# Shared down products of four expert layers as three fp32r products

## The reference, cut to what matters

```
g = einsum('bsh,hi->bsi', x, gate_w)
u = einsum('bsh,hi->bsi', x, up_w)
return einsum('bsi,ih->bsh', gelu(g, approximate=True) * u, down_w)   # h = 128, i = 512
```

## Time and profile before

| what | value |
|---|---|
| median of 3 runs | 1442.39 us (1441.62 to 1445.08) |
| the profiled execution | 1442.76 us |
| its span, first to last instruction | 1440.9 us |
| PE busy | 1248.3 us, 87% |
| DVE busy | 856.1 us, 59% |
| ACT busy | 710.7 us, 49% |
| POOL busy | 269.1 us, 19% |
| mean granted clock of PE | 0.96 of full speed |

### The profile page before, as it was taken

How to read it: one execution, slowest core, us unless ns; L and a number is a source line. 1 busy time by engine, 2 the same in 40 slices (tenths; PEclk the granted TensorE clock), 3 DMA queues, 4 the chain that set the end, 5 groups by cost and what they waited for, 6 DMA issues and landing times.

```text
span 1440.9 us, 26352 instructions
## 1 busy us (share of the span) xinstructions
PE 1248.3 (87%) x9301; PEld 967.7 (67%) x9301; DVE 856.1 (59%) x1800; ACT 710.7 (49%) x1385; POOL 269.1 (19%) x454
## 2 busy tenths in 40 slices
PE   4799960678988889998988999989999998998989
PEld 2455620346877779887777888589888854456867
DVE  4878669654445466657776445466564566664242
ACT  1556668545445434444444445333434376665554
POOL 1899200000001213330000003043320111100000
PEclk9899985799999999999999999999999999999999
DMA  8000010211050213212205200123120000000000
GB/s 304 1 2 2 2 73 0 116 81 59 1 198 10 90 56 102 56 29 96 110 1 210 88 1 25 48 80 88 36 94 1 1 1 2 2 2 1 0 15 15
DMA packets 42607, 75.71 MB, mean 53 GB/s; under 512 B 3817, under 2 KB 33521, under 8 KB 41585
## 3 DMA queue, kind: packets, MB, share of 16 engines
q1 hardware_dynamic: 38384, 65.62, 12.5%
q0 software_dynamic: 4096, 8.40, 2.0%
HBM read 59.72 MB, written 14.29 MB: 51 GB/s over the span
## 4 chain that ended last, share of the span: by engine, by line
PE 67%; DVE 15%; ACT 9%; issue 5%; POOL 2%; DVEq 1%; DMA 1%; ACTq 0%; SPq 0%; POOLq 0%
PE bank L1635 7%; PE bank L1624 7%; PE bank L1620 6%; PE bank L1679 5%; PE bank L1413 3%; PE bank L1479 3%; PE bank L1689 3%; PE bank L1611 3%; PE bank L1418 3%; PE bank L1420 2%; PE bank L1419 2%; PE bank L1604 2%; PE bank L1606 2%; PE bank L1605 2%; PE bank L1529 2%
## 5 line engine op out<-in xcount | busy, mean ns | idle before, releaser
L1872 ACT ACTIVATE SC<-bank 128x512 f32<-128x512 f32 x192 | 114.1, 596 | 220.4 <-PE bank L1620 130.3
L1959 DVE SCALAR_TENSOR_TENSOR SC<-bank,SM,SC 128x512 f32<-128x512 f32 x128 | 95.9, 749 | 142.6 <-PE bank L1624 119.7
L2549 POOL DMA_INDIRECT xs<-CC,POSI x64 | 63.6, 994 | 536.1 <-DVE POSI L2353 234.0
L1635 PE MATMUL bank<-A,SC 128*128 x1024 | 137.1, 277 | 10.5 <-DVE SC L1959 9.6
L1624 PE MATMUL bank<-X,SC 128*128 128x128 f32 x1024 | 137.3, 277 | 6.1 <-DVE SC L2234 5.8
L1620 PE MATMUL bank<-X,SC 128*128 128x128 f32 x1024 | 137.5, 278 | 2.0 <-ACT SC L1856 2.0
L1635 PEld LDWEIGHTS bank<-A,SC 128*128 128x128 f32 x1024 | 125.4, 192 | 20.2 <-issue 19.4
L1620 PEld LDWEIGHTS bank<-X,SC 128*128 128x128 f32 x1024 | 128.5, 195 | 14.4 <-issue 12.5
L1624 PEld LDWEIGHTS bank<-X,SC 128*128 128x128 f32 x1024 | 125.4, 193 | 8.2 <-DVE SC L2234 8.1
L1679 PE MATMUL bank<-A 128*128 128x128 f32 x736 | 99.6, 279 | 11.8 <-DVE A L2374 8.1
L1772 ACT ACTIVATE A<-bank,SM 128x128 f32<-128x128 f32 x256 | 73.6, 383 | 66.0 <-DVE SM L2055 65.7
(11 more groups left out here) (319 smaller groups left out, 2570.3 us busy)
## 6 DMA issues: line engine op xcount, KB each, us to landing
A<-in_moe SPq DMA_DIRECT2D x36, 768.0 KB, 10.2
A<-xs SPq DMA_DIRECT2D x20, 256.0 KB, 3.4
ys<-A SPq DMA_DIRECT2D x20, 256.0 KB, 2.4
BW<-in_l1f SPq DMA_DIRECT2D x2, 2048.0 KB, 7.8
BW<-in_l2f SPq DMA_DIRECT2D x1, 3456.0 KB, 12.0
BW<-in_l1c SPq DMA_DIRECT2D x1, 3072.0 KB, 17.0
BW<-in_l3f SPq DMA_DIRECT2D x1, 2816.0 KB, 9.5
A<-in_l1c SPq DMA_DIRECT2D x1, 2560.0 KB, 8.6
```

The source lines that it names most:

```text
L1635: m = e.matmul(o, at["h"].ap[:, cut(q)], W[:, bass.ds(r + (1024 + 128 * q), 128)], start=k == 0 and q == 0, stop=k == 1 and q == 3)
L1872: e.activation(at["h"].ap, at["pg"].ap, ACT.Gelu_apprx_tanh).then_inc(at["gelu"][0], 1)
L1959: return e.scalar_tensor_tensor(out=o, in0=a, scalar=s, in1=b, op0=o1, op1=o2)
```

## The change

- The shared down product of each (layer, chunk, m) becomes three fp32r products of 512 columns: high weights by high block, high weights by low block, low weights by high block.
- A new stage `hs` stands between `h0` and `h1` of each shared item. In it ACT copies the inner block as fp32r (the high part) and DVE writes block minus high part over the block. The down product comes one round later.
- `split_down` makes high and low parts of the down weights, once a layer (one ACT copy, one DVE subtraction of 128 x 512), at four places beside other items.
- The constants CC get an fp32r name over the same memory. High parts lie in free columns of BW and CC; moe1's high weights, the scan sums NM and DN, and the second attention's probabilities (out of RS into two slots of CC) move to other columns.
- The load `l1g` moves two items later, and waits for moe1's last shared down product.

The diff, with context lines left out:

```diff
@@ -143,7 +143,6 @@
...
-        CC = sb("CC", CW)
@@ -155,11 +154,12 @@
...
-                nc.sbuf_tensor("WT8", [128, 1024], F32) as WT8:
+                nc.sbuf_tensor("WT8", [128, 1024], F32) as WT8, nc.sbuf_tensor("CC", [128, CW], F32) as CC:
...
+        RCC = sb("RCC", CW, F32R)
@@ -217,7 +217,13 @@
...
-        MOE_HI = {"moe1": RBW[:, 6912:7936], "moe2": RW8[:, :], "moe3": RW8[:, :], "moe4": RW8[:, :]}
+        MOE_HI = {"moe1": RBW[:, 6144:7168], "moe2": RW8[:, :], "moe3": RW8[:, :], "moe4": RW8[:, :]}
+        MOE_HID = {"moe1": RBW[:, 7168:7680], "moe2": RBW[:, 2560:3072], "moe3": RBW[:, 6912:7424], "moe4": RBW[:, 6912:7424]}
+        CA, CQ = CL["As0"][0], CL["q1"][0]
+        HH1 = Ring([RBW[:, 7680:8192], RCC[:, CA:CA + 512]])
+        HH2 = Ring([RBW[:, 3072:3584], RCC[:, CQ:CQ + 512]])
+        HH3 = Ring([RBW[:, 7424:7936], RCC[:, CQ:CQ + 512]])
+        HHI = {"moe1": HH1, "moe2": HH2, "moe3": HH3, "moe4": HH3}
@@ -735,6 +741,7 @@
...
+            RSM = Ring([CC[:, CA + 512 * k:CA + 512 * k + 512] for k in (1, 2)])
@@ -759,7 +766,7 @@
...
-                    at = step("a1_max", pa=u["pa"], mm=u["mm"], s=RS.take(), m=sm(4))
+                    at = step("a1_max", pa=u["pa"], mm=u["mm"], s=RSM.take(), m=sm(4))
@@ -777,7 +784,7 @@
...
-                    RS.give(u["s"], at["tr"])
+                    RSM.give(u["s"], at["tr"])
@@ -805,6 +812,11 @@
...
+
+        def split_down(name, after):
+            at = step("sh_wdown", L=name, after=after)
+            at["hi"], at["lo"] = tick("moe_act"), tick("moe_vec")
+            sig["shared_wd", name] = at["lo"]
@@ -834,18 +846,29 @@
...
+                    def hs(n=n, m=m, u=u):
+                        if name == "moe1" and (n, m) == (1, 0):
+                            HH1.slots[1] = Slot(RBW[:, 4096:4608])
+                            HH1.slots[1].over = sig["l1c_over"]
+                        k = RS.slots.index(u["h"].slot)
+                        at = step("sh_split", h=u["h"], ready=u["t"], hh=HHI[name].take(), lo=RSC[:, 512 * k:512 * k + 512])
+                        at["hi"], at["t"] = tick("moe_act"), tick("moe_vec")
+                        u.update(hh=at["hh"], lo=at["lo"], t=at["t"])
+
...
-                        at = step("sh_down", L=name, n=n, m=m, h=u["h"], ready=u["t"], pc=pc["s"], yfree=sig["Yfree", n])
+                        at = step("sh_down", L=name, n=n, m=m, hh=u["hh"], lo=u["lo"], w=sig["shared_wd", name], ready=u["t"],
+                                  pc=pc["s"], yfree=sig["Yfree", n])
...
+                        HHI[name].give(u["hh"], at["mm"])
...
-                    out_items.append(([(in_key, n)], [hx, h0, h1], None))
+                    out_items.append(([(in_key, n)], [hx, h0, hs, h1], None))
@@ -1043,7 +1066,7 @@
...
-                    at["copy"] = u["copy"] = tick("ffn_vec")
+                    at["copy"] = u["copy"] = sig[wname + "_copied"] = tick("ffn_vec")
@@ -1154,7 +1177,7 @@
...
-        NM, DN = BW[:, 6912:7428], BW[:, 7428:7944]
+        NM, DN = BW[:, 1024:1540], BW[:, 1540:2056]
@@ -1334,12 +1357,15 @@
...
-        beside(items, 18, 1, [lambda: split_weights("moe1", [sig["down"]])])
+        beside(items, 18, 1, [lambda: (split_weights("moe1", [sig["down"]]), split_down("moe1", [sig["down"]]))])
...
+        beside(f1[5][1], 22, 1, [lambda: split_down("moe2", [sig["l1f_copied"]])])
...
+        beside(m2, 43, 1, [lambda: split_down("moe3", [sig["l1f_last"]])])
+        beside(m3, 46, 1, [lambda: split_down("moe4", [sig["moe3_shared_over"]])])
...
-        put(m1, 42, action(("x1", 3), lambda: load("l1g", sig["moe1_up_over"])))
+        put(m1, 44, action(("x1", 3), lambda: load("l1g", sig["moe1_shared_over"])))
@@ -1605,11 +1631,13 @@
...
-                    a, m = SW + 1024 + 128 * at["m"], at["m"]
+                    a, m, hi = SW + 1024 + 128 * at["m"], at["m"], MOE_HID[at["L"]][:, cut(at["m"])]
...
+                    w.wait_ge(*at["w"])
...
-                    e.matmul(at["pc"].ap, MOE_AT[at["L"]][:, a:a + 128], at["h"].ap, start=m == 0,
-                             stop=m == 3).then_inc(at["mm"][0], 1)
+                    e.matmul(at["pc"].ap, hi, at["hh"].ap, start=m == 0, stop=False)
+                    e.matmul(at["pc"].ap, hi, at["lo"], start=False, stop=False)
+                    e.matmul(at["pc"].ap, MOE_LO[at["L"]][:, a:a + 128], at["hh"].ap, start=False, stop=m == 3).then_inc(at["mm"][0], 1)
@@ -1862,6 +1890,15 @@
...
+                elif kind == "sh_wdown":
+                    w.wait_ge(*loaded[at["L"]])
+                    for s in at["after"]:
+                        w.wait_ge(*s)
+                    e.activation(MOE_HID[at["L"]], MOE_AT[at["L"]][:, SW + 1024:SW + 1536], ACT.Copy).then_inc(at["hi"][0], 1)
+                elif kind == "sh_split":
+                    over(at["hh"])
+                    w.wait_ge(*at["ready"])
+                    e.activation(at["hh"].ap, at["h"].ap, ACT.Copy).then_inc(at["hi"][0], 1)
@@ -2219,6 +2256,15 @@
...
+                elif kind == "sh_wdown":
+                    a = SW + 1024
+                    w.wait_ge(*loaded[at["L"]])
+                    w.wait_ge(*at["hi"])
+                    e.tensor_tensor(MOE_LO[at["L"]][:, a:a + 512], MOE_AT[at["L"]][:, a:a + 512], MOE_HID[at["L"]],
+                                    ALU.subtract).then_inc(at["lo"][0], 1)
+                elif kind == "sh_split":
+                    w.wait_ge(*at["hi"])
+                    e.tensor_tensor(at["lo"], at["h"].ap, at["hh"].ap, ALU.subtract).then_inc(at["t"][0], 1)
```

## The result

| | before | after |
|---|---|---|
| median | 1443.74 us (4 runs, 1441.62 to 1445.10) | 1463.86 us (4 runs, 1460.61 to 1465.24) |
| ratio | | 1.0138, 95% interval 1.0122 to 1.0154 |
| profiled execution, its span | 1442.76, 1440.9 us | 1460.61, 1458.8 us |
| PE at half clock, within the span | 116.1 us | 137.9 us |
| mean granted clock | 0.960 | 0.953 |

A forecast was written before the change was run, and what follows sets the result against it. PE was taken as the bound in the fourth layer, with DVE or ACT ending stalls in most other chunks. 1442.76 + 0.6 + 1.4 = 1444.8 us, set to 1444.4 us against the median; range 1436 to 1451.5 us.

The forecast's parts named there:

- the clock's: Stalls behind the router grow to 3.6 us; one more drop to half speed taken, +1.4 us, bounds -2.8 and +8.4.
- Rival two: All four scan and four router chunks run at half speed, six drops more, 8.4 us: 1451.4 us; chance 0.27.
- The sum without clock: All gains and losses in the expert layers before any clock drop: +0.6 us, nearly nothing left of 10.9 us saved.
- three plain chunks (moe4, 1 to 3): Fourth layer's chunks without a stall keep their gain of 4 x 0.17 = 0.7 us each: -2.0 us.
- four scan chunks: Chunks with scan inputs: PE's first idle stretch grows from 1.5 to about 2.4 us; +0.34 us each, +1.4 us.
- combining at a start (moe2, moe4, chunk 0): First chunks of layers two and four: the first down product also waits for DVE's subtraction; +1.0 us each, +2.0 us.
- router behind the first expert (moe1, moe3, chunk 1): Second chunks of layers one and three: fewer products ahead of an unlengthened chain; -0.5 us each, -1.0 us.
- router ahead of m = 3 (moe1, moe3, chunks 2 and 3): Router before the last up product: +0.25 us a chunk, -0.3 where layer one's second exp holds PE; together -0.1 us.
- moe1, chunk 0: Layer one's first chunk, beside the second attention: +0.3 us, taken between -0.7 (no stall) and +1.0 (combining).
- Moves, `l1g`: Moved buffers are only changes of address, and the later load still arrives 28 us before its first read: 0.
- rival three: In the down products, each fp32r product costs 0.43 us, three take 1.29: 27 us slower; chance under 0.01.
- Rival one: PE bounds the expert layers after all: 10.9 us go, 1431.5 us, or 1437 if stalls keep half; chance 0.18.

The follow-up runs named there:

- late_only: The kernel after without block or weight splits and with float32 down products; moved buffers, later load and late round with an empty stage stay; 1.0012 of the kernel before.
- warm_after: The kernel after with bf16 products that add nothing put into PE's stalls in the expert layers; 1.0011 of the kernel before, repeated 1.0007.
- moves_only: The kernel after with float32 down products in their old round and no splits; only moved buffers and the later load stay; 0.9999 of the kernel before.
- no_split_work: The kernel after without block copy and subtraction: DVE's fp32r-rounded product feeds all three products, low part left out; 0.9941 of the kernel before.

## Why the prediction was wrong

**The step that failed is the clock's**: "I take one more, +1.4 us; bounds -2.8 (none drops) and +8.4". In the profiled execution seven further stretches at half speed came, worth 10.5 us in the expert layers; by the ratios the clock cost 16 us. The number of drops was wrong, not the price of one.

- *How many.* I let the router and scan chunks drop, eight at most with two there already. Of these eight, six did, four of them anew (the router chunk at 866.9, the scan chunks at 662.1, 744.0 and 785.0). The three other stretches came where I had thought of none: in moe1's first two chunks, behind waits of 2.42 and 1.93 us for d0's subtraction. One of the two at 351.5 belongs to the late round: `late_only`, without any split, has a fall at 350.6 too.
- *From how long a stall.* Rival two held the scan chunks near danger at 2.4 us idle. They idled 2.04 to 2.24 us and three of four dropped; 1.93 us from 392.4 on sufficed, and 3.38 us in moe1 did not. The length of the stall alone does not decide it. The Trainium skill (TensorE: Matmul & The Clock Gate, section What's actually happening) says that the gate's window runs free of the kernel; the pairs 2.23 and 2.24 us with and without a drop agree.
- *What one costs.* 1.4 us was taken without a working: the one down product that I had read showed 1.0 us. It was luck that it held, for 1.3 to 1.8 us are measured. I let layer one's last chunk off, because ACT's second exp holds PE there anyway; its fall costs nothing.

Rival two named the right mechanism and its place. Its 1451.4 us had six further drops at 1.4 us; seven came in one execution, some ten by the clocks of all runs, and the rest of the sum was too low as well.

**The sum without clock** was +0.6 us. By the ratios of the two kernels with filled stalls it is 4.2 us, and by their chunks 6.0 (growth in the second table, for the last chunks of moe1 and moe3 up to the last expert product):

| step | forecast | measured |
|---|---|---|
| three plain chunks (moe4, 1 to 3) | -2.0 | +0.09, -0.66, -0.65 = -1.2 |
| four scan chunks | +1.4 | 1.16 + 0.60 + 1.23 + 0.90 = +3.9 |
| combining at a start (moe2, moe4, chunk 0) | +2.0 | 0.80 + 0.80 = +1.6 |
| router behind the first expert (moe1, moe3, chunk 1) | -1.0 | 0.98 - 0.19 = +0.8 |
| router ahead of m = 3 (moe1, moe3, chunks 2 and 3) | -0.1 | -0.09 + 0.13 - 0.68 + 0.09 = -0.6 |
| moe1, chunk 0 | +0.3 | +1.45 |

- *Plain chunks*: right where nothing else stands (0.66 and 0.65 for 0.68). Chunk 1 isn't plain: combining goes on in it. A window that reads "134.76 of 135 us busy" doesn't say that no chain runs close.
- *Scan chunks*: the step "PE's first idle stretch grows from 1.5 to about 2.4 us" was near (2.04 to 2.24), and the direction right. Left out was the second chain of the chunk, with its 0.84 us: in `warm_after` that second wait is 1.31 us, since a subtraction stands there too.
- *Router*: "lasts 3.6 us", ended by the new subtraction. Measured 3.37 to 3.45. Right.
- *Combining*: right in size.
- *Moves, `l1g`*: costed at nothing, and `moves_only` shows nothing. Right.
- *The fp32r products*: 0.69 for 0.86 us, right; rival three falls.
- *Rival one* (PE the bound after all) falls for the kernel after. `no_split_work` shows that it was the split that stood against it: 0.9941, some 8.5 us gained over the kernel before.

Why moe1's chunk 0 grew by 1.45 us is not settled, nor what makes the time between the layers vary from one execution to the next. Nor was it tried whether the split could be made without a handover between ACT and DVE.

## What to carry to other kernels

Where an engine's stalls are set by others, taking work off it makes them longer, and each may cost clock on top: price a further fall at the chunk with it less the same chunk without it (here 1.3 to 1.8 us), not by a product or a sibling chunk, and let it come at every stall of two microseconds, also those that you judged harmless. A quick test is to fill the stalls with products that add nothing, in the old kernel and in the new one; the difference of the two is the change without the clock. A part that is worth a few microseconds is better read from the chunks that hold it than from the ratio of whole runs. And ask of work added "beside" an engine in which chains it will stand: here 1.3 us of copy and subtraction were free in plain rounds and cost 12 us in the chains.

## What was not expected of the hardware

- A wait of 1.93 us was followed by half clock, one of 3.38 us was not, in the same execution. The fall can come when PE works again: it resumed at 394.37 us, and the clock fell at 395.9.
- A fall cost 1.3 to 1.8 us in the eight places read in two kernels, and nothing in moe1's last chunk. There a third table load (at 480.97 us in the kernel before) makes PE wait behind the fall anyway, 0.40 and 0.93 us before the next expert products; that this absorbs the fall is a reading of the trace, not tested.
- The products that fill the stalls, some 0.23 us each (2.78 us for twelve), slow nothing that shows: with them the kernel before gains 0.2 to 0.5%.
- A product handed from DVE to ACT and back takes 0.73 and 0.66 us from start to start for instructions of 0.69 and 0.63 us; the handover itself adds 0.04 and 0.03 us, and it is the standing in line that costs.
